# Gram stage of a graph network layer: one of four rows of a chunk scaled and shifted on GpSimd, its ReLU folded into VectorE's addition

## The reference, cut to what matters

```python
h = relu(layernorm(x));  x = x + gnn0(h, W, src, dst, edge_weight)   # layer 0: one product, 25000 edges
h = relu(layernorm(x));  x = x + gnn1(h, src, dst, W1, b1, gamma, beta, W2, b2)

def gnn1(x, ...):                      # x: 50000 nodes x 256
    agg = segment_sum(x[src], dst)     # 25000 edges
    h  = agg + x
    h1 = h @ W1 + b1                   # 256 -> 1024
    h1 = (h1 - mean(h1)) * rsqrt(var(h1) + eps) * gamma + beta      # over all 50000 nodes
    return relu(relu(h1) @ W2 + b2)
```

## Time and profile before

| | |
|---|---|
| median of 3 timed executions | 3873.82 us (3873.27 to 3875.31) |
| profiled execution | 3883.61 us, its span 3881.8 us |
| Gram stage, from the first ReLU that never waits to the last of a full chunk | 1391.42 to 1660.04 us |
| granted TensorE clock over the span | 0.947 of full speed |
| busy over the span | PE 88%, DVE 58%, ACT 56%, POOL 27% |

### The profile page before, as it was taken

How to read it: one execution, slowest core, us unless ns; L and a number is a source line. 1 busy time by engine, 2 the same in 40 slices (tenths; PEclk the granted TensorE clock), 3 DMA queues, 4 the chain that set the end, 5 groups by cost and what they waited for, 6 DMA issues and landing times.

```text
span 3881.8 us, 56824 instructions
## 1 busy us (share of the span) xinstructions
PE 3433.2 (88%) x17113; PEld 2909.6 (75%) x17113; DVE 2267.4 (58%) x5129; ACT 2162.8 (56%) x3533; POOL 1033.6 (27%) x801
## 2 busy tenths in 40 slices
PE   0378887488877779999999999999999999999999
PEld 0368877477766657778888888888888888888888
DVE  0366665376565668855555555555555655555555
ACT  0255554232222279956666666666666666666665
POOL 6667777688888710000000000000000000000000
PEclk9888888698888889999999999999999999999999
DMA  9988786577777799934333334333333343343342
GB/s 337 335 204 191 191 196 134 121 175 164 161 158 156 160 314 359 360 128 128 111 113 130 108 114 129 108 116 127 108 121 122 108 125 118 110 126 115 112 125 69
DMA packets 305854, 619.82 MB, mean 160 GB/s; under 512 B 34997, under 2 KB 186800, under 8 KB 299856
## 3 DMA queue, kind: packets, MB, share of 16 engines
q1 hardware_dynamic: 229440, 515.46, 39.9%
q0 software_dynamic: 75264, 102.81, 15.5%
q10 hardware_dynamic: 1072, 0.76, 0.1%
HBM read 412.83 MB, written 257.28 MB: 173 GB/s over the span
## 4 chain that ended last, share of the span: by engine, by line
PE 58%; POOL 18%; issue 11%; ACT 6%; another core or an unknown queue 3%; DMA 2%; DVE 1%; ACTq 0%; POOLq 0%; DVEq 0%
PE ps_a L1286 28%; PE ps_b L1300 19%; PE ps_b L1301 9%; POOL x_table L552 7%; POOL agg_table L552 7%; ACT late L685 4%; POOL edge_tiles L542 4%; DMA x_table<-edge_tiles,scatter_now 2%; POOL edge_ring L542 1%; ACT late_r L703 1%; DMA agg_table<-edge_tiles,scatter_now 1%; ACT edge_tiles L631 0%; PE ps_b L1204 0%; DVE edge_same L847 0%
## 5 line engine op out<-in xcount | busy, mean ns | idle before, releaser
L1300 PE MATMUL ps_b<-w_hl,late_r 128*128 128x512 f32 x3128 | 1129.0, 396 | 0.0
L749 ACT ACTIVATE hid<-ps_a,bn_bias,bn_scale 128x512 f32<-128x512 f32 (+1 forms) x784 | 609.1, 777 | 734.9 <-PE ps_a L1286 734.9
L1129 DVE TENSOR_TENSOR late_r<-hid,late_r 128x512 fp32r<-128x512 f32 (+1 forms) x784 | 537.3, 685 | 815.0 <-ACT late_r L754 815.0
L1286 PE MATMUL ps_a<-late_r,w_hi 128*128 128x512 f32 x3136 | 984.0, 395 | 0.0
L1301 PE MATMUL ps_b<-w_hl,late_r 128*128 128x256 f32 x3128 | 876.3, 280 | 0.0
L1300 PEld LDWEIGHTS ps_b<-w_hl,late_r 128*128 128x128 f32 x3128 | 587.6, 188 | 138.9 <-issue 0.5
L1286 PEld LDWEIGHTS ps_a<-late_r,w_hi 128*128 128x128 f32 x3136 | 540.5, 188 | 108.9
L1286 PE MATMUL ps_a<-late_r,w_lo 128*128 128x512 f32 x1568 | 611.8, 390 | 0.0
L1301 PEld LDWEIGHTS ps_b<-w_hl,late_r 128*128 128x128 f32 x3128 | 590.0, 189 | 26.4
L754 ACT ACTIVATE late_r<-hid 128x512 fp32r<-128x512 f32 (+1 forms) x784 | 494.8, 631 | 71.7
L1215 PE MATMUL ps_b<-edge_tiles,edge_same 128*128 128x256 f32 x1568 | 404.2, 423 | 0.0
(11 more groups left out here) (122 smaller groups left out, 4391.3 us busy)
## 6 DMA issues: line engine op xcount, KB each, us to landing
x_rows<-x_table SPq DMA_DIRECT2D x291, 512.0 KB, 4.4
late<-agg_table SPq DMA_DIRECT2D x194, 512.0 KB, 5.7
x_table<-in_x SPq DMA_DIRECT2D x10, 5000.0 KB
agg_table<-zeros SPq DMA_DIRECT2D x40, 1250.0 KB
hT_table<-h_turned SPq DMA_DIRECT2D x388, 128.0 KB, 2.5
hT_f<-hT_table SPq DMA_DIRECT2D x97, 512.0 KB, 3.6
out<-zeros SPq DMA_DIRECT2D x97, 512.0 KB, 6.8
x_table<-edge_tiles,scatter_now POOLq DMA_INDIRECT x196
```

The lines of the kernel that those rows point to most:

```text
L749: act.activation(hid[m % 2][:, 0:w].rearrange("p (r a b) -> p r a b", a=BANDS, b=SQUARE), by_row, ACT.Relu, scale=bn_scale[:, m:m + 1], bi ...
L1129: dve.tensor_tensor(hid_lo[m % 4][:, 0:w], hid[m % 2][:, 0:w], hid_hi[m % 4][:, 0:w].bitcast(F32), ALU.subtract).then_inc(hid_lo_ready, 1)
L1286: ins = pe.matmul(ps_a[:, 2 + m % 2, 0:w], w_part[:, kb, cols], h_part[:, kb * w:(kb + 1) * w], start=(t == 0), stop=(t == len(terms) - 1))
L1300: pe.matmul(ps_b[:, r, :], hid_hi[m % 4][:, cols], w2, start=(m == 0), stop=(m == MB - 1), skip_group_check=True)
```

## The change

ScalarE now does the first three of a chunk's four rows (two of three in the last chunk). The row left over goes to GpSimd, as a multiplication and an addition with the same scale and shift, without the ReLU, into the same slot of `relu_ln`. VectorE's addition becomes one instruction that takes the maximum with 0 first and then adds, over all rows; for the three rows that went through ScalarE's ReLU the maximum changes nothing. It waits for GpSimd's row too. The main stage, whose own code also has such rows, is not touched.

```diff
+        gram_last_row = sem("gram_last_row")
...
+            def gram_norm(t):
+                s, (p, j) = t.slot(2), shape_of(t.n)
+                r = j - 1
+                pool.wait_ge(norm_picked, t.n + 1)
+                pool.wait_ge(gram_x_loaded[t.slot(LOADS)], t.use(LOADS) * 16 + 16)
+                pool.wait_ge(gram_h, t.n + LOADS - 1)
+                pool.sem_inc(pool_gate, 1)
+                pool.tensor_scalar(relu_ln[s][0:p, r, :], x1_in[t.slot(LOADS)][0:p, r, :], norm_now[s][0:p, 0, r:r + 1],
+                                   norm_now[s][0:p, 1, r:r + 1], ALU.mult, ALU.add).then_inc(gram_last_row, 1)
+            turns(pool, CHUNKS, 0, 4, gram_norm)
...
             def relu_norm(c, s, load):
                 p, j = shape_of(c)
-                for r in range(j):
+                for r in range(j - 1):
                     ins = act.activation(relu_ln[s][0:p, r, :], x1_in[load][0:p, r, :], ACT.Relu,
...
                 dve.wait_ge(gram_relu, t.n + 1)
+                dve.wait_ge(gram_last_row, t.n + 1)
                 dve.wait_ge(gram_a_loaded[t.slot(LOADS)], t.use(LOADS) * 16 + 16)
                 dve.wait_ge(gram_lo, t.n + 1)
-                dve.tensor_tensor(h[s][0:p, 0:j, :], relu_ln[s][0:p, 0:j, :], agg_in[t.slot(LOADS)][0:p, 0:j, :],
-                                  ALU.add).then_inc(gram_h, 1)
+                dve.scalar_tensor_tensor(h[s][0:p, 0:j, :], relu_ln[s][0:p, 0:j, :], 0.0, agg_in[t.slot(LOADS)][0:p, 0:j, :],
+                                         ALU.max, ALU.add).then_inc(gram_h, 1)
```

## The result

The changed kernel takes 3863.84 us (median of 8 executions, 3860.88 to 3867.82), the kernel before in the same sessions 3875.88 us (8 executions, 3873.27 to 3878.03). The ratio is 0.9971 with a 95% interval of 0.9962 to 0.998: 0.3% faster, 12 us, where 13 us were forecast. The profiled execution took 3864.24 us, its span 3862.4 us.

What follows compares the result with a forecast made beforehand. ScalarE was taken to bound the Gram stage at 2.92 us a chunk. VectorE's 2.43 + 0.35 for GpSimd's row = 2.78 would be the new beat; 92 chunks x 0.14 = 13 us gave 3861 us, range 3847 to 3888.

Steps and rivals of the forecast that it cites:

- The bound: Gram stage: ScalarE never waits and sets 2.92 us a chunk; one ACTIVATE less makes it 2.44, no longer the limit.
- The addition's form: VectorE's addition with the maximum: 1220 ns against 1226 for the plain addition, so zero cost.
- The added wait: VectorE's addition also waiting for GpSimd's row: put at 0, if the row is there in time.
- The hold: GpSimd's row makes VectorE's large instructions stand still: 0.35 us a chunk, bounded by 0 and 0.99.
- VectorE's own beat: VectorE's time for a Gram chunk with nothing to wait for: 1.29 + 1.14, together 2.43 us.
- a longer hold of 0.49 us decides: Gram stage: the change turns slower from a GpSimd delay of 0.49 us a chunk, where 2.43 + 0.49 = 2.92.
- TensorE's ring: Rounding of chunk t + 2 waits for the matmuls of chunk t: 5.26 us for two chunks, taken as 2.66 each.
- The loads: Loads of the Gram stage: 394 GB/s needed at 2.66 us a chunk; 358 is no ceiling, since 408 was seen.
- No hold: Rival, 25%: GpSimd reads and writes beside VectorE without delaying it; TensorE sets 2.66 us a chunk, 3850 us.
- The slower cases: Rival, 20%: a dearer GpSimd row or a late VectorE; 0.70 us gives 3893 us, 0.99 gives 3920.

Runs made afterwards that it cites:

- before_h4g4: Kernel before, without the change, with four buffers of h and four slots of gram_in instead of two: beat 2.919 us, 3881.89 us.
- row_beside: Changed kernel with all four rows on ScalarE again and GpSimd's row into an unused buffer, still waited for: ratio 1.0001 to the kernel before, beat 2.920 us.
- no_row: Changed kernel without GpSimd's row, the fourth row a constant 0: 3866.54 us, ratio 0.9954 to the kernel before, beat 2.719 us.
- row_twice: Changed kernel with a second GpSimd row of 256 columns into an unused buffer ahead of the real one: beat 3.000 us, 3894 us.
- row_wide: Changed kernel with an extra GpSimd row of 512 columns into an unused buffer ahead of the real one: beat 3.217 us, 3912 us.
- row_memset: Changed kernel with a GpSimd memset of 256 columns, which reads nothing, ahead of its row: beat 2.777 us.
- h4g4: Changed kernel with four buffers of h and four slots of gram_in instead of two: 3858.64 us, ratio 0.9928 to the kernel before, beat 2.627 us.
- late_row: Changed kernel with GpSimd's row released by VectorE's rest instead of by the copies: beat 2.807 us, 3876.75 us.
- h4g4_no_row: Changed kernel with four buffers of h, four slots of gram_in and a constant 0 for GpSimd's row: beat 2.560 us, 3850.79 us.

## Why the prediction was right, and where its sum was not

**The bound.** Right. ScalarE set the beat before (before_h4g4, row_beside: 2.92 with four rows whatever else is changed), and one ACTIVATE less freed it.

**The addition's form.** Right, zero.

**The added wait.** Right: no addition waited for GpSimd's row. It ends at 1503.93 in the rows above, and the addition of its chunk starts at 1506.46.

**The hold.** The mechanism is right and shown: a row that reads delays VectorE (no_row, row_twice, row_wide), one that only writes doesn't (row_memset). Its size was taken too large: 0.35 us was the term, in the changed kernel it is 0.14, and where nothing covers it 0.20 to 0.23 (h4g4, late_row, row_twice). By my estimate GpSimd keeps VectorE out for some 0.27 us from the end of the rest (0.13 of gap and 0.14 of a longer addition), not for the whole 0.56 us of its instruction.

**VectorE's own beat.** This step failed. "Two large instructions with nothing to wait for start 1.14 apart" was read from an addition followed by a rest. The other way round there is a wait: the addition reuses the buffer of `h` that the rest just ahead reads (`gram_lo`), and starts 1.34 or 1.35 us after it. The last two rows don't show it, but the next one in the trace would have, 1.35 us after the rest at 1663.27:

```profile
1664.62 0.96 DVE L1015 TENSOR_TENSOR late<-late 112x768 f32<-112x768 f32 x1
```

It is a faint hint, since ScalarE's rows for this addition end only at 1664.53 (1662.95 + 1.58), 0.09 us ahead of it; in before_h4g4, which has no such wait, the same addition starts 0.03 us after them. The gap is shown by the changed kernel, by no_row without GpSimd (never under 1.32 us), and by h4g4, where it is 1.14. So VectorE's own beat is 1.29 + 1.35 = 2.64, not 2.43. The two errors cancel: 2.43 + 0.35 = 2.78 was forecast, 2.64 + 0.14 = 2.78 is what it is. The right total is in part luck, and the verdict "a longer hold of 0.49 us decides" was too lenient: from 2.64 it decides at 0.28.

**TensorE's ring.** Named rightly as the limit next in line, put at 2.66, measured at 2.72 (no_row). I had only closed the ring over two chunks. There is a longer ring beside it: rounding of chunk t, rows of t + 2, their addition, the rest of t + 1, the matmuls of t + 1, rounding of t + 3. It does not explain the difference. In no_row the roundings at 1450.20 and 1458.18 are three chunks apart, 2.66 us each, but the beat is not even there: the starts of the additions repeat in fours, some 2.64, 2.64, 2.77 and 2.81 us apart. The traces have one link that differs by chunk. In the kernel before, two additions of each four start 0.03 or 0.04 us after the end of ScalarE's rows and the other two 0.20 to 0.23; in no_row one of four starts 0.03 us after them and two 0.20 to 0.22. A delay of 0.18 in two chunks of four is 0.09 a chunk, enough for the missing 0.06 (an estimate; no run tests it), and what causes it is open. TensorE's own pace was mis-sized as well: 2.53 (h4g4_no_row), not 2.63.

**The loads.** Right: 377 GB/s in the changed kernel, 400 with the larger buffers. The share of 0.98 before was no ceiling. At 410 GB/s in h4g4_no_row they may be the limit.

**The rivals.** No hold is refuted by row_twice and row_wide. The slower cases needed a dearer row; it is not dearer.

## What to carry to other kernels

Before work is moved to an idle engine, ask what the engine shares with the one that becomes the next bound: here work on the idle GpSimd costs VectorE 0.8 ns for each column that GpSimd reads, and nothing for what it only writes or while VectorE waits anyway. Take an engine's own beat from a place where each pair of its instructions follows in the same order as in the loop, and look for waits of the engine on itself, since a buffer that is reused at once costs a gap that busy shares don't show. When the first bound is gone, deeper buffers that were worth almost nothing before may be worth as much as the change.

## What the runs showed of the hardware

In these traces VectorE's instructions with two inputs in SBUF and GpSimd's reading instructions hold up one another. GpSimd's row takes 0.56 us alone and 1.2 with a rest in its way, and 2.2 us where VectorE leaves no gap: there GpSimd was passed over between a rest and an addition that follow at 1.14 us, and came in at the small copies. One of these, with a single input, was held too (0.38 us instead of 0.16).

The Trainium skill ("SBUF — State Buffer", "Summary: rules for kernel authors") has the second of the two instructions blocked until the first finishes. For GpSimd behind one VectorE instruction the trace agrees. VectorE behind GpSimd is free earlier. At the start of the stage GpSimd's row ran from 1382.46 to 1383.02, and VectorE's rest started behind it:

```profile
1382.69 1.40 DVE L1038 TENSOR_TENSOR late_r<-late,late_r 128x1024 fp32r<-128x1024 f32 x1 [0.96 <-ACT late_r L715]
```

It lasted 0.19 us longer than the 1.21 of the others, where a block up to GpSimd's end would have been 0.33.

A wait of VectorE for the signal of its own previous instruction moves the next start from 1.14 us behind it (h4g4) to 1.34 or 1.35 (the changed kernel).
